# A gated cross-attention and FFN block on one core: the words of two steady steps in a new order

## The reference

```python
x = x + tanh(g_xattn) * attention(layernorm(x), ctx, ctx, wq, bq, ..., wo, bo)   # 16 heads of 16, softmax over 375
# the FFN on layernorm(x):
router_probs = softmax(xt @ router_w)                      # 8 experts
top_k_probs, top_k_indices = top_k(router_probs, 2)
top_k_probs = top_k_probs / sum(top_k_probs)
combine = einsum('tk,tke->te', top_k_probs, one_hot)
expert_out = gelu(xt @ w1 + b1) @ w2 + b2                   # 256 -> 1024 -> 256
out = expert_out * sum(combine, axis=-1)
x = x + tanh(g_ffn) * out
```

## Time and profile before

| | |
|---|---|
| median of 3 runs | 709.57 us (709.5 to 710.0) |
| profiled execution, span | 1105.9 us |
| mean granted TensorE clock in it | 0.556 |
| PE busy | 1088.8 us |
| DVE busy | 526.6 us |
| ACT busy | 408.3 us |
| POOL busy | 329.7 us |

### The profile page before, as it was taken

One profiled execution on the slowest core, in us unless ns is written; L12 is line 12 of the kernel. 1 busy time (PEld: TensorE's weight loads), 2 busy tenths in 40 slices (PEclk: granted clock), 3 DMA queues, 4 the chain that ended last, 5 costly groups with the idle time before them and its releaser, 6 DMA issues.

```text
span 1105.9 us, 20672 instructions
## 1 busy us (share of the span) xinstructions
PE 1088.8 (98%) x7648; PEld 972.5 (88%) x7648; DVE 526.6 (48%) x1299; ACT 408.3 (37%) x797; POOL 329.7 (30%) x474
## 2 busy tenths in 40 slices
...
GB/s 189 187 124 140 78 99 31 74 69 74 99 52 71 52 74 99 52 95 28 74 98 52 117 14 83 82 64 110 42 61 70 74 99 52 63 24 10 2 10 17
DMA packets 47797, 80.27 MB, mean 73 GB/s; under 512 B 10997, under 2 KB 30802, under 8 KB 47698
## 3 DMA queue, kind: packets, MB, share of 16 engines
...
## 4 chain that ended last, share of the span: by engine, by line
PE 97%; SPq 1%; DVE 1%; DMA 0%; POOL 0%; issue 0%; ACT 0%; POOLq 0%
PE P L951 48%; PE S L980 13%; PE OT L1010 12%; PE T L992 12%; PE P L1036 4%; PE TR L1019 2%; PE TR L1095 2%; PE TR L1026 1%; PE TR L1078 1%; PE TR L1063 1%; SPq L430 1%; PE TR L966 1%; DMA CTRAW<-in_ctxT 0%; DVE NEGM L783 0%; POOL CT_LO L591 0%
## 5 line engine op out<-in xcount | busy, mean ns | idle before, releaser
L783 DVE TENSOR_REDUCE NEGM<-S 112x1 f32<-112x375 f32 x512 | 272.3, 542 | 186.5 <-PE S L980 181.9
L703 ACT ACTIVATE PROBS<-T 125x448 f32<-125x448 f32 x384 | 204.2, 543 | 208.1 <-PE T L992 199.7
L980 PE MATMUL S<-KS,QS 96*112 96x376 f32 x512 | 239.6, 484 | 1.7 <-DVE NEGM L783 1.7
L992 PE MATMUL T<-QS,KS 98*125 98x224 f32 x768 | 209.1, 376 | 0.0
L992 PEld LDWEIGHTS T<-QS,KS 98*125 98x125 f32 x768 | 169.6, 244 | 22.9 <-issue 7.1
L1010 PE MATMUL OT<-PROBS,VA 125*17 125x112 f32 x3072 | 140.1, 364 | 0.0
L980 PEld LDWEIGHTS S<-KS,QS 96*112 96x112 f32 x512 | 118.3, 239 | 19.1 <-issue 10.2
L1010 PEld LDWEIGHTS OT<-PROBS,VA 125*17 125x17 f32 x3072 | 107.4, 128 | 21.0 <-issue 9.3
L606 POOL CAST HT_HI<-HG 128x224 fp32r<-128x224 f32 x124 | 45.9, 370 | 256.5 <-ACT HG L729 255.1
L729 ACT ACTIVATE HG<-P,B 128x224 f32<-128x224 f32 x128 | 57.3, 447 | 123.2 <-PE P L951 123.2
L951 PE MATMUL P<-W_HI,HT_LO 128*112 128x256 f32 x256 | 98.9, 386 | 0.0
(11 more groups left out here) (112 smaller groups left out, 1817.5 us busy)
## 6 DMA issues: line engine op xcount, KB each, us to landing
...
KS<-KLO SPq DMA_DIRECT2D x128, 94.0 KB, 2.7
CTRAW<-in_ctxT SPq DMA_DIRECT2D x32, 375.0 KB, 3.3
...
```

Of the source, the lines that this page charges most:

```text
L703: act.activation(PT[0:KN, k, pp * 4 * SQ:(pp + 1) * 4 * SQ], T_BANK[i % 2][0:KN, 0:4 * SQ], ACT.Exp, scale=SCALE).then_inc(exp_done, 1)
L783: dve.tensor_reduce(NEGM[:, b.par, col:col + 1], S_BANK[i % 2][0:SQ, 0:SK], AX.X, ALU.max, negate=True).then_inc(max_done, 1)
L980: pe.matmul(S_BANK[i % 2][0:SQ, 0:SKP], QS[0:96, b.gpar, i % 2, i // 2, b.j * SQ:(b.j + 1) * SQ], KS[0:96, b.ring, i // 2, :], start=True, ...
L992: mm = pe.matmul(T_BANK[i % 2][0:KN, r * 2 * SQ:(r + 1) * 2 * SQ], KS[0:98, prv.ring, pair, k * KN:(k + 1) * KN], QS[0:98, prv.gpar, :, pa ...
```

## The change

`ORDER` and `SPECIAL` are written anew, no other line. Over the whole run the same words are done for the same batches. The first entry of `ORDER` now holds nearly all words of a pair of steps (those of the odd step with a lateness one or two higher or, as -1, one ahead), and the second only `ct+1`. `SPECIAL[5]` gives up the words that the new list of step 6 takes over, `SPECIAL[32]` takes those that the last pair leaves; the others are only broken into lines in another way. All four pv of a batch now stand side by side in both steps, one set behind `x2t`, the other between `n1` and `n2`. The T products of both batches are spread between S products, up, dh, dn and the projections. `ct` of the even batch stands at the end, behind lo.7 and xb. `rt` stands ahead of `x2t` of the same pair: the router product then reads what `xt` left in XT. Its weights sum to one whatever they are, so that only rounding depends on it, and its work is as large as before.

```diff
 ORDER = [stages(text) for text in (
-    """st.5+1 dh.0+2 s.11+1 n2+1 dn.0+2 st.6+1 wo+1 x2n+2 st.7+1 s.12+1 st.8+1 dh.1+2 st.9+1 dn.1+2 kd.0+1
-       x2t s.13+1 st.10+1 s.14+1 kd.1+1 ql+1 k.0 k.1 s.15+1 st.11+1 lo.0 rt pv.0+1 pv.1+1 xn rx rw.0 rw.1
-       pv.2+1 mt cl+1 pv.3+1 rw.2 rw.3 s.0 up.0 m s.1 up.1 s.2 up.2 lo.1 s.3 au+1 up.3 s.4 up.4 lo.2 s.5
-       kd.0 up.5 s.6 lo.3 lo.4 up.6 s.7 xl n1 ct s.8 up.7 s.9 v.2+1 ct-1 st.0 s.10 st.1 kd.1 s.11 rw.4 v.0
-       s.12 lo.5 xt s.13 v.1 cl st.2 s.14 st.3 v.2 lo.6 rw.5 st.4 s.15 ol+1 rw.6 q.0 st.5 s.0-1 st.6 q.1""",
-    """mt st.7+1 s.1 st.8+1 s.2 k.0 st.9+1 st.10+1 s.3 k.1 st.11+1 pv.0+1 pv.1+1 pv.2+1 l1-1 pv.3+1 m s.4
-       au+1 rw.7+1 s.5 st.0 v.0 n2+1 s.6 st.1 s.7 v.1 st.2 st.3 s.8 s.9 n1 wo+1 st.4 s.10 qs+1 lo.7+1 xb+2""")]
+    """rw.3+2 au+2 st.0+1 st.1+1 rw.4+2 s.5+1 s.6+1 dh.0+2 n1+1 ct+1 st.2+1 s.7+1 wo+2 n2+1 rw.5+2 st.3+1 rw.6+2
+       kd.1+2 st.4+1 rw.7+2 rx s.8+1 m+1 v.0+1 rt rw.0 st.5+1 dn.0+2 s.9+1 st.6+1 st.7+1 s.10+1 wo+1 s.11+1
+       st.8+1 x2n+2 s.12+1 dh.1+2 st.9+1 st.10+1 s.13+1 dn.1+2 s.14+1 st.11+1 l1 s.15+1 k.0 cl+2 k.1 x2t kd.0+1
+       pv.0+1 pv.1+1 pv.2+1 pv.3+1 up.0 s.0 rw.1 mt up.1 lo.0 s.1 s.2 lo.1 up.2 lo.2 s.3 xn rw.2 up.3 up.4 lo.3
+       s.4 up.5 s.5 kd.1+1 s.6 up.6 au+1 s.7 lo.4 up.7 st.0 s.8 cl+1 v.1+1 s.9 lo.5 s.10 st.1 v.2+1 qs+2 ql+1
+       s.11 xt v.0 lo.6 st.2 s.12 v.1 st.3 s.13 st.4 m s.14 v.2 st.5 s.15 st.6 q.0 kd.0 xl s.0-1 st.7 k.0-1
+       s.1-1 q.1 mt-1 st.8 s.2-1 st.9 k.1-1 s.3-1 st.10 s.4-1 st.11 n1 xb+1 pv.0 lo.7 pv.1 ol+1 pv.2 pv.3 n2""",
+    """ct+1""")]
...
-    (5, """mt cl+2 st.7+1 s.1 st.8+1 k.0 s.2 rw.0+1 lo.7+1 st.9+1 st.10+1 rw.1+1 l1-1 rw.2+1 rw.3+1 k.1 s.3 ct
-       st.11+1 kd.0+1 kd.1+1 cl+1 pv.1+1 pv.2+1 pv.3+1 s.4 au+1 v.2+1 s.5 st.0 st.1 s.6 v.0 m s.7 st.2 s.8
-       st.3 rw.4+1 wo+1 st.4 qs+1 n1 rw.5+1 rw.6+1 s.9 xb+2 v.1 rw.7+1 s.10"""),
+    (5, """mt cl+2 st.7+1 s.1 st.8+1 k.0 s.2 rw.0+1 st.9+1 st.10+1 rw.1+1 rw.2+1 k.1 s.3 st.11+1 kd.0+1 pv.1+1 pv.2+1
+       pv.3+1 s.4 lo.7+1 v.2+1 xb+2"""),
...
```

More of the change, by code:

```diff
@@ L81 @@
+    """ct+1""")]
 SPECIAL = {k: stages(text) for k, text in (
     (-3, """"""),
-    (-2, """zp zq zr ld.3 zi wk ld.2 zh cx wq l1 xn tg ld.1 wv k.0 k.1 xt ct v.0 bo ka.0 ld.0 l1-2 q.0 ld.5 q.1
-       xn-2 xt-2 ld.4 ld.6 v.1 w.0 v.2"""),
+    (-2, """zp zq zr ld.3 zi wk ld.2 zh cx wq l1 xn tg ld.1 wv k.0 k.1 xt ct v.0 bo ka ld.0 l1-2 q.0 ld.5 q.1 xn-2 xt-2
+       ld.4 ld.6 v.1 w.0 v.2"""),
     (-1, """k.0 l1-3 ct v.0 wl xn-3 lw.0 k.1 q.0-1"""),
-    (0, """s.0 s.1 cl+3 q.1 s.2 zy v.1+1 s.3 s.4 s.5 on+1 s.6 v.2+1 s.7 s.8 k.0 s.9 s.10 k.1 s.11 ld.7 qs+2 v.0
-       s.12 ct xl s.13 v.1 w.1 s.14 s.15 kd.1+2 ql+1 v.2 cl+2 s.0-1"""),
@@ L88 @@
[L88 to L100, removed]
@@ L101 @@
-    (5, """mt cl+2 st.7+1 s.1 st.8+1 k.0 s.2 rw.0+1 lo.7+1 st.9+1 st.10+1 rw.1+1 l1-1 rw.2+1 rw.3+1 k.1 s.3 ct
-       st.11+1 kd.0+1 kd.1+1 cl+1 pv.1+1 pv.2+1 pv.3+1 s.4 au+1 v.2+1 s.5 st.0 st.1 s.6 v.0 m s.7 st.2 s.8
-       st.3 rw.4+1 wo+1 st.4 qs+1 n1 rw.5+1 rw.6+1 s.9 xb+2 v.1 rw.7+1 s.10"""),
[L104 to L111, removed]
+    (0, """s.0 s.1 cl+3 q.1 s.2 zy v.1+1 s.3 s.4 s.5 on+1 s.6 v.2+1 s.7 s.8 k.0 s.9 s.10 k.1 s.11 ld.7 qs+2 v.0 s.12 ct
+       xl s.13 v.1 w.1 s.14 s.15 kd.1+2 ql+1 v.2 cl+2 s.0-1"""),
```

20 lines of the change are left out of this document (added).

## The result

| | median | range, runs |
|---|---|---|
| before | 711.93 us | 709.50 to 719.66, 16 |
| changed | 718.03 us | 715.73 to 724.54, 16 |

The ratio is 1.0085, 95% interval 1.0054 to 1.0116: the change costs about 6 us. 701 was forecast, and 718 lies above 716, the upper end of the range.

What follows compares the result with a forecast made beforehand. The prediction took PE as the bound in the profile, with DVE setting some stretches in timed runs. Gains of 2 + 1 + 5 + 0.5 = 8.5 us from 709.57 gave 701 us, range 693 to 705.

Steps and rivals of the forecast that it cites:

- The bound: PE bounds the profiled run; in timed runs 0 to 5.8 us of each pair is PE waiting that an order can recover.
- The sign that the prediction set itself: Prediction is wrong if timed PE is not near its upper level or its waits differ from those DVE's shares indicate.
- (a): Even step's V product no longer split by mt: 0.1 to 0.2 us gained a pair, 1 to 3 us in all.
- (b): V product and transposes side by side on PE, ten blocks become eight: 0.1 us gained a pair, about 1 us.
- (c): DVE's load spread more evenly over a pair: 0.4 us gained a pair, bounds 0 and 0.8; 5 us in all.
- (d): ACT relieved by spreading the odd step's T products: 0.05 us a pair, under 1 us; router's exponent wait covered.
- (e): ct moved to the end of POOL's list lands between 0.15 us late and 1.8 us early; costed at nothing.
- (f): SP's kd, qs, ql, cl and m change places: cost nothing, bound 3.3 us a pair.
- rival 3: Slower by POOL: k.0 of the odd step waits 1.0 us a pair for ct; 720 us, chance 0.17.
- Rival 4: Slower by the clock: joined V product and transposes bring PE to its lower level once a pair; 736 us, chance 0.08.
- the rule on transposes: Trainium skill: the fast clock does not engage for transposes, so those beside a V product would lengthen the low-clock stretch.
- Rival 1: Only PE's own stream gains, DVE's excess being hidden by the S banks: 706.5 us, chance 0.22.

Runs made afterwards that it cites:

- The repeated run: The kernel before, unedited, timed and profiled once more: 711.72 us, ratio 0.9992, profiled span 709.0 us at a mean granted clock of 0.990.
- x3: The kernel before with mt moved out of the even step's V product to behind s.0: 717.72 us, ratio 1.0083.
- y1: The kernel before with mt moved out of the even step's V product to behind up.0: 708.52 us, ratio 0.9956.
- x4: The changed kernel with st.3, s.15 and st.11 moved between kinds of PE work that stood side by side: 716.55 us, ratio 1.0066 to before.
- x2: The kernel before with xn moved from behind pv.1 to behind s.3: 711.87 us, ratio 0.9981.
- x1: The changed kernel with xn moved from behind s.3 to between pv.1 and pv.2: 712.91 us, ratio 1.0017 to before.
- y3: The changed kernel with rw.1 and rw.2 moved into the even step's V product, xn left behind s.3: 715.79 us, ratio 1.0060 to before.

## Why the prediction was wrong, by its own steps

**The bound, where it failed.** Two facts were put together: the timed runs take 0.642 of the profiled span, and PE at full clock would take 0.556 of it. The 5.8 us a pair in between were then taken for PE's waiting in timed runs. The repeated run shows the step that fails: PE's own time goes with 0.619, not 0.556, because an `up` word goes from 1.08 to 0.66 us and a V product from 4.07 to 2.42. So 41.55 - 37.3 = 4.2 of the 5.8 us were PE's own work, but for 0.41 us of waits. The other 1.5 (43.1 - 41.55) came from spreading the ratio of the whole run, 0.642, over the pairs: these shorten to 0.619, and so the start and the end to more than 0.642. In the steady pairs the view of waits lists none for an S maximum. The sign that the prediction set itself, that it is wrong if PE's waits are not those that DVE's shares point to, is what came.

**(a) Unsplit V product.** Right in sign and nearly in size: forecast 0.1 to 0.2 us a pair, and 0.23 in x3 and y1, 3 us in all. In the changed kernel the V product also runs in one piece, from 395.47 to 397.89, but its edges come to as much as before. The price of `mt` "between 0 and 0.19" held only because its new place is behind `up.0`; ahead of `up.0` it cost 0.67 us of waits in the kernel before (x3). That was luck: the table load was in no term.

**(b) Fewer blocks.** Wrong in sign: a gain of 0.1 was forecast, and the other edges grew by 0.25 if (a) saves in the changed kernel the 0.23 that it saves in y1 (edges 1.97 against 1.95). Counting blocks was the wrong measure. What is paid is paid at every passage between two kinds, and between transposes and V product as well: `wo` ahead of `n2` costs 0.19 us, `x2t` ahead of V 0.17. x4, which puts the words apart again, changes it by 0.03.

**(c) DVE.** The term that carried the forecast, and the step that made it wrong in sign: +0.4 us a pair, 0.8 at most. It came out as -0.81. Three things failed.

First, there was nothing to take away. The steady pairs before have no listed wait for an S maximum, and only 0.41 us of waits of any kind.

Second, DVE's busy share of a stretch didn't show where PE waits. The heaviest stretch of the new order by the prediction's sum, `s.8` to `st.4`, and the one in which the 0.41 us are lost, `s.1` to `s.5` (`s.6` starts at 403.59), in the changed kernel:

```profile
405.58:410.73 5.15, 5.15 (x44) 5.09 (x43) 4.34 (x10) 3.98 (x8) 4.91 (x8) 1.00 0.55 168
399.60:403.59 3.99, 3.74 (x31) 3.48 (x30) 3.76 (x10) 2.17 (x5) 3.67 (x8) 1.00 0.37 88
```

In the first, DVE is busy 4.34 of 5.15 us, 84%, and PE waits for nothing. In the second, DVE is busy 94%; taken 5 us wide, which is what the prediction's windows of 8 us come to at the upper clock, it is 87% (4.34 of the 5.00 us from 398.60), hardly more than in the first. This stretch was in no sum of the prediction. It holds three reduces, two XN and PR between the reduces of `s.0` and `s.4`, with two S banks to lag by.

Third, the sum took DVE's instructions at their means of the kernel before. XN and PR stand beside POOL's `lo` in the new order and take 1.33 us for two XN instead of 0.73, and 0.32 instead of 0.15 us for PR. x2 has the late `xn` in the same 8 us and costs nothing, as said there.

x1 and y3 show 0.41 of the 0.81 us at this one place; the rest, in pieces of 0.1 us and less, I have not attributed one by one, and for it the cause stays open.

**(d) ACT.** Its 0.05 us a pair didn't show. The waits for the exponent of T fell by 1.2 us in all, but in the last pair; the steady pairs had none to relieve. The router's exponent ahead of `rt` did hardly any harm, 0.04 us at `st.7`.

**(e) POOL.** Right that it costs nothing. `ct` at the end meets a late transfer, and POOL waits for it much longer than before, 116.7 us in 14 waits against 47.9. Nothing of it reaches PE: no wait for CT_LO in the steady steps.

**(f) SP.** Right, by the same waits: the later transfer shows as POOL's wait alone.

**The rivals.** The time came near rival 3 (720 us), but not by its way. Rival 4, the clock, is shown wrong: at a V product with its transposes, and from the start-up to the end, the granted clock is 1.00:

```profile
394.70:398.00 3.30, 3.30 (x104) 2.94 (x103) 1.84 (x4) 2.33 (x4) 0.89 (x2) 1.00 0.00 0
45.00:722.00 677.00, 668.79 (x7541) 633.83 (x7539) 486.74 (x1250) 379.48 (x780) 307.26 (x450) 1.00 0.38 107
```

The transposes gain by the clock as other work does: the four of `xt` take 0.32 us at 1.00 and took 0.50 at 0.556. So the rule on transposes that the prediction set against itself isn't borne out here.

Rival 1, that only PE's own stream gains because PE is the bound, had the right picture of the bound and was given 0.22; even it lacked a price for what a new order can lose. Its gain of 3 us is what y1 reached with part (a) alone. What was missing was a rival "slower, by DVE": a fixed order in which PE waits for almost nothing has more to lose than to gain.
